# One expert phase of a two-layer kernel: folding steps between more gathers, and a wait ahead of each later fetch

## The reference

```python
# one expert part: x (4096, 128); gate_w (8, 128); wi_gate, wi_up (8, 512, 128); wo (8, 128, 512)
N = B * S; capacity = int(N / E * 1.25)                    # 4096 tokens, 640 slots for each of 8 experts
router_probs = softmax(x_flat @ gate_w.T)
top_k_probs, top_k_idx = top_k(router_probs, 2)            # renormalised to a sum of 1
for k in range(2):                                          # first choice, then second choice
    eid, ew = top_k_idx[:, k], top_k_probs[:, k]
    pos = rank of the token among those with this eid       # a cumulative sum
    valid = pos < capacity
    disp[e, pos] = x_flat                                   # tokens gathered by expert
    gate = silu(disp @ wi_gate.T); up = disp @ wi_up.T
    expert_out = (gate * up) @ wo.T
    out += where(valid, ew * expert_out[eid, pos], 0)
# the whole: x = x + 0.5 * experts(layernorm(x)); x = x + attention(layernorm(x)); x = x + 0.5 * experts(layernorm(x))
# the attention part: q, k, v through causal convolutions of 4 taps and silu, a delta rule over chunks of 32,
# convolutions of 3, 15 and 31 taps on v, mixed per head, a small gate network, rms norm and an output product
```

## Time and profile before

| | |
|---|---|
| median of 3 runs | 924.49 us (923.41 to 927.39) |
| profiled execution, first to last instruction | 984.4 us |
| what lies around that span in the profiled execution | not recorded; the span is all that is known of its time |
| PE busy | 868.5 us (88%) |
| DVE, POOL, ACT busy | 544.8, 502.9, 398.8 us |
| mean granted PE clock | 0.935 of full speed |

### The profile page before, as it was taken

How to read it: one execution, slowest core, us unless ns; L and a number is a source line. 1 busy time by engine, 2 the same in 40 slices (tenths; PEclk the granted TensorE clock), 3 DMA queues, 4 the chain that set the end, 5 groups by cost and what they waited for, 6 DMA issues and landing times. The chain is left out here.

```text
span 984.4 us, 26269 instructions
## 1 busy us (share of the span) xinstructions
PE 868.5 (88%) x10885; PEld 762.7 (77%) x10885; DVE 544.8 (55%) x1645; ACT 398.8 (41%) x858; POOL 502.9 (51%) x631
## 2 busy tenths in 40 slices
PE   8375999999869788998999889988987899999996
PEld 7255999989867566786678666866676799999996
DVE  5643656655447944666485734473445256566553
ACT  5622444433314322374436622661253334444441
POOL 2658889456530721582138512882144433445667
PEclk8677999999989898999999998998897989999998
DMA  9342587444113110012001300111011624435544
GB/s 309 105 114 65 185 263 227 124 127 127 52 54 85 23 36 11 4 28 55 8 4 34 86 26 25 30 32 52 28 42 57 227 79 147 135 119 117 121 85 46
DMA packets 75475, 85.97 MB, mean 87 GB/s; under 512 B 9767, under 2 KB 62163, under 8 KB 74332
## 3 DMA queue, kind: packets, MB, share of 16 engines
q1 hardware_dynamic: 61148, 63.74, 21.4%
q0 software_dynamic: 14208, 20.55, 8.8%
HBM read 46.70 MB, written 34.01 MB: 82 GB/s over the span
## 5 line engine op out<-in xcount | busy, mean ns | idle before, releaser
L1020 DVE TENSOR_TENSOR e_hid<-e_sg,e_pu 128x320 f32<-128x320 f32 x256 | 124.9, 488 | 189.4 <-ACT e_sg L961 137.0
L961 ACT ACTIVATE e_sg<-e_pg 128x320 f32<-128x320 f32 x256 | 111.5, 438 | 234.1 <-PE e_pg L918 175.0
L916 PE MATMUL e_pg<-e_xlo,e_whi 128*128 128x320 f32 x256 | 97.5, 381 | 17.3 <-DVE e_hid L1020 7.6
L282 POOL DMA_INDIRECT queue<-wide_rows,slot x64 | 67.7, 1058 | 72.1 <-ACT wide_rows L568 22.2
L1112 POOL TENSOR_TENSOR first_rows<-a_inv,a_nmat 128x135 f32<-128x135 f32 (+20 forms) x116 | 59.9, 516 | 71.6 <-DVE a_nmat L1962 63.5
L904 PE MATMUL e_po<-e_expert,e_hid 128*128 128x128 f32 x640 | 84.1, 275 | 5.8 <-DVE e_rows L994 4.5
L904 PE MATMUL e_po<-expert,e_hid 128*128 128x128 f32 x640 | 85.4, 277 | 2.9 <-DVE e_rows L994 2.9
L904 PEld LDWEIGHTS e_po<-e_expert,e_hid 128*128 128x128 f32 x640 | 79.7, 191 | 7.1 <-DVE e_rows L994 5.3
L904 PEld LDWEIGHTS e_po<-expert,e_hid 128*128 128x128 f32 x640 | 81.0, 193 | 4.0 <-DVE e_rows L994 3.7
L917 PE MATMUL e_pg<-e_xhi,e_wlo 128*128 128x320 f32 x256 | 80.1, 313 | 0.0
L918 PE MATMUL e_pu<-e_xhi,e_whi 128*128 128x320 f32 x256 | 80.0, 312 | 0.0
(11 more groups left out here) (379 smaller groups left out, 2132.6 us busy)
## 6 DMA issues: line engine op xcount, KB each, us to landing
expert<-wexp_in SPq DMA_DIRECT2D x14, 512.0 KB
e_expert<-wexp_in SPq DMA_DIRECT2D x14, 512.0 KB
line<-blank SPq DMA_DIRECT2D x3, 1310.0 KB
e_xs<-queue SPq DMA_DIRECT2D x12, 327.5 KB, 4.6
e_xs<-line SPq DMA_DIRECT2D x6, 647.5 KB, 5.8
expert<-wexp_in SPq DMA_DIRECT2D x14, 256.0 KB
e_expert<-wexp_in SPq DMA_DIRECT2D x14, 256.0 KB
queue<-blank SPq DMA_DIRECT2D x2, 1310.0 KB, 9.7
```

Of the source, the lines that this page charges most:

```text
L282: pool.indirect_dma_start(io.queue, bass.IndirectOffsetOnAxis(ap=k.slot[:, j, 1:2], axis=0), k.xn[:, j, :], None, bounds_check=SLOTS - 1, ...
L916: pe.matmul(out, whi[par][:, i, fs], xlo[par][:, cols], start=True, stop=False)
L961: act.activation(sg[n % 2][:], pg[n % 2][:, 0:HALF], ACT.Silu).then_inc(silued, 1)
L1020: dve.tensor_tensor(hid[q % 2][:, f, c * HALF:c * HALF + HALF], sg[n % 2][:], pu[n % 2][:, 0:HALF], ALU.mult).then_inc(hidden, 1)
```

## The change

There are two parts. The first puts a folding step behind every second gather already in queues 0 to 2; the count goes over the gathers of all three. Six folding steps so move ahead of queue 3, and everything behind them takes later steps of the same list. The second puts a wait ahead of each fetch: fetch n behind queue q waits until gate step n of phase q + 2 is done. The function `pick` goes.

```diff
-            def pick(q):
-                rows_read(pool, q - NX)
-                pick_rows(pool, io.table, k, q, rows_of(q), 0 if q else OPEN_TILES, CT, picked[q % NX] if q else first)
...
                 folding = raw.folding(pool, k, folded)
                 for q in range(3):
-                    pick(q)
+                    for n in range(0 if q else OPEN_TILES, CT):
+                        pick_rows(pool, io.table, k, q, rows_of(q), n, n + 1, picked[q] if q else first)
+                        if (q * CT + n) % 2 == 0:
+                            next(folding)
                 sent = EARLY
...
+                fetched = 0
                 for q in range(E, NQ):
                     keep_tiles(CT * q, CT * q + CT)
-                    fetch(sum(FETCHED_WITH[:q - E]), sum(FETCHED_WITH[:q - E + 1]))
+                    for n in range(FETCHED_WITH[q - E]):
+                        pool.wait_ge(hidden, NB * (q + 2) + n + 1)
+                        fetch(fetched, fetched + 1)
+                        fetched += 1
```

## The result

The changed kernel took 929.79 us (median of 12 runs, 925.54 to 935.77), the kernel before 924.25 us beside it (12 runs, 919.13 to 929.47): a ratio of 1.0058, 95% interval 1.0038 to 1.0077. It is slower. The prediction had 917.0 us and faster; its first rival, "the stall is not in the timed runs", had 929.4 us.

The account below looks back on a forecast made before the run. PE, busy 88% of the 984.4 us span, was taken as the bound, with gains only where it stands. Turn(7)'s 7.5 us, other terms at nothing, taken from the timed 924.5 gave 917.0 us; range 913 to 930.

Parts of the forecast that it names:

- first rival: Stall of phase 0 absent from timed runs, so the change is 4.9 us slower, 929.4 us; chance 0.30.
- turn(7) term: PE's turn to queue 7's rows in e1: at 144.2 in place of 151.73, a gain of 7.5 us.
- turn(1): PE's transposes of queue 1's rows: usable at 74.7, PE held 1.8 us more, phase 1 at 77.3 for 88.36.
- turn(2): PE's turn to queue 2's rows: usable at 82.3, with a new PE wait of 3.1 us.
- The price of a product ahead of a gather: On POOL in e1: each folding product moved ahead of a gather delays it by 0.99 us.
- The landing: Time from issue of a queue's last gather until its rows are usable: taken as 3.0 us, between 2.5 and 4.2.
- The clock: PE's clock may fall again at the waits of turn(1) and turn(2); up to 1.6 us hides at turn(7).
- The weight split: DVE splits beside POOL's folding steps in phases 0 and 1: 4.7 us at most, taken as nothing.
- First delivery: POOL comes to its first delivery as early as before; 3.4 us of its 10.89 us wait for DVE are left.
- Part two: Waits ahead of 16 fetches: gates already open, cost 0, and phase 10 keeps its 1.72 us over phase 2.
- Rivals two and three: Two: the stall stays, 924.5 us, chance 0.22. Three: gates spread the fetches in phases 10 to 14, 908.4 us, chance 0.04.

Follow-up runs that it names:

- e0: The kernel before, unchanged, profiled a second time: 924.14 us, ratio 0.9998.
- e5: The changed kernel with 32 small filler products on PE ahead of turn(1): 927.68 us, ratio 1.0028 to the kernel before.
- e2: The kernel before with part two alone, a wait on a gate step ahead of each fetch: 923.77 us, ratio 0.9985.
- e9: The kernel before with a folding step behind every gather of queues 3 and 4 in place of every second: 936.67 us, ratio 1.0109.
- e10: e9 with the four blanking writes on SP issued one phase earlier: 929.02 us, ratio 1.0035 to the kernel before.
- e11: The kernel before with the four blanking writes on SP one phase earlier and nothing else: 925.07 us, ratio 0.9998.
- e15: e9 with only the blanking write behind queue 7's last gather issued one phase later: 932.22 us, ratio 1.0090 to the kernel before.

## Why the prediction was wrong

- **The failed step** is the baseline of the turn(7) term: "Before, turn(7) was at 151.73: a gain of 7.5 us", with the difference between span and timed runs taken "over whole". Counted from the first gather, 151.73 is 95.31; two undisturbed profiles of the same kernel have 82.75 and 82.65. The 12.6 us between are the stall of the earlier trace rows. It is in neither of these profiles, whose own times are those of the timed runs, while the forecast needed more than 4.9 us of it to be there for any gain at all. The term then reads 87.11 - 82.75 = 4.4 us lost in place of 7.5 won. The stall was also taken for an effect of long rows of gathers; seven kernels with the same row and no stall speak against that.
- **The range.** 929.79 lies inside 913 to 930, but only because the upper end was drawn to take in part of the first rival. The forecast itself, 917.0, had the wrong sign. Its lower end is also miscounted: with a landing of 2.5 us the last gather at 141.2 is usable at 143.7, so turn(7) could not come at 142.1, and the end is 916.5, not 914.9.
- **The first rival had it.** It put before's turn(1), turn(2) and turn(7) at 72.9, 78.0 and 139.3, which are 16.5, 21.6 and 82.9 behind the gather at 56.42; e0 has 15.56, 21.98 and 82.75. Its loss of 4.9 is 4.2 at turn(15) and 5.5, 3.1 and 3.8 us in the three timed comparisons, so that 929.4 fell within 0.4 of the measured 929.79 is in part chance. It was given 0.30 against 0.42, though the gap of 59.9 us between span and median was named as the reason for it. A row that no dependency explains, in a profile whose span is 6% over the timed runs, was kept because it was visible.
- **turn(1), turn(2).** Predicted at 74.7 and 82.3, that is 18.3 and 25.9 behind the first gather; measured 18.30 and 25.89. That they fit to the hundredth is luck, two errors against each other: the last gathers came 0.9 and 0.5 us earlier than predicted (14.37 and 22.39 for 15.3 and 22.9), and the landings took 0.9 and 0.5 us longer. The baseline of queue 1's gather was the disturbed profile's, 12.29 behind the first, where e0 has 11.51. The price of a product ahead of a gather, 0.99, measured 0.91 to 1.04 (2.16 to 2.29 us from gather to gather, less 1.25).
- **The landing** was taken as 3.0, between 2.5 and 4.2. Measured 3.93, 3.50 and 3.77 at the three turns: nearer the upper end.
- **turn(7).** Last gather predicted at 141.2, 84.8 behind the first; measured 83.34. The six moved steps cost 4.4 at it in place of 4.9, a figure that its named parts don't give: four pairs at 0.84, with the other two steps read as roundings at 0.41, are 4.2. With the longer landing this came to 87.1 for 87.8.
- **The clock.** The low clock behind the first wait was real (PE's transposes took 1.33, phase 0's mean is 0.72) and hidden, as e5 shows, but in the wait at turn(2) and not at turn(7). Behind turn(2) it did not fall (12.11 us to turn(3) at 1.00); the wait there was 1.02 us, where 3.1 had been predicted.
- **The weight split.** Taken as nothing, and so it was: the four L975 of phases 0 and 1 take 3.14 us together after and 3.15 in e0. The row of 1.86 us in the earlier trace rows is there again in e0 (1.85). In both it is the DVE product that started first, some 0.27 us ahead, and was stretched, while POOL's step took its usual 1.03: a row that shows the two in each other's way, but not that the second one waits.
- **First delivery.** In e0 POOL comes to it with 0.79 us of idle time and a folding step as what it waited for, so the cover of 10.89 us in the earlier trace rows was the stall's too. The changed kernel has 5.30, as DVE is later and the folding is not:

```profile
182.53 1.05 POOL L341 DMA_INDIRECT token<-e_rows,e_token  x1 [5.30 <-DVE e_rows L994]
```

```profile
183.01 1.06 POOL L341 DMA_INDIRECT token<-e_rows,e_token  x1 [0.79 <-POOL lag_lo L259]
```

- **Part two.** Right: the gates are open, cost 0 (e2). But "the 1.72 us that phase 10 has over phase 2 stay" was wrong for the same reason as the main step: undisturbed, phase 10 has none, before and after.
- **Rivals two and three** fall: phase 0 did not end as before, and e2 moved no phase.

## What to carry to other kernels

Before a stall in a profile becomes a term of a sum, compare the span with the timed runs: if it is several per cent longer, that execution is not the one to be improved, and stalls that no dependency explains are the first to strike. Work moved ahead of a transfer is paid in full where the rows are wanted as soon as they land, here 0.9 to 1.0 us a product at the queues for which PE waits already. And a small gather should be issued well ahead of a bulk transfer of the next phase, since being late can cost more than the delay: in e9 the last gather of queue 7 was issued only 1 us later than in the changed kernel, and its rows were used 7.9 us behind the issue in place of 3.8.

## What the runs showed of the hardware that was not expected

- One profiled execution of three was 63 to 67 us longer than the other two of the same kernel (spans of 984.4 against 921.2 and 917.5), with idle time of ACT and DVE that "remote" ended; its cause is open.
- The time from the issue of a queue's last gather to its use went with what other transfers were under way. With the next write of 1310 KB 2.5 to 3.0 us behind the gather it was 3.7 to 3.8 us, with 1.64 us 3.9 in e9 and 5.8 in e10, where the DMA share was 1.04 to 1.07 in the 4 us ahead of it, 9.7 behind three writes of 1024 to 1310 KB (e11), with 0.16 us 7.9 (e9), and 4.5 once that write was taken away (e15).
- Filling PE's wait at turn(1) kept its granted clock at the upper level of 2.4 GHz (five transposes 0.77 us in place of 1.33), and the fall to 1.2 GHz came at the next wait of 2.79 us instead.
- The start of the stage moved between 54 and 58.5 us from one execution to the next, as much as the effect studied; only times counted from the first gather can be compared.
